# A twelve-sublayer decoder on one core: TensorE's filler products are taken out

## The reference, cut to what matters

```
x = x + sublayer(layernorm(x))
```

## Time and profile before

| what | value |
|---|---|
| median of 3 runs | 4220.63 us (4219.37 to 4225.47) |
| the profiled execution | 4219.39 us, span 4217.6 us |
| PE busy (share of the span) | 3372.7 us (80%), 18289 products |
| DVE, ACT, POOL busy | 2078.1, 1146.6, 401.5 us |
| mean granted TensorE clock | 0.892 |
| filler products (L108) | 1016, 280.9 us busy |
| one batch of the early loop | 727.0 us (777.57 to 1504.55) |
| one batch of the late loop | 249.3 us (3474.11 to 3723.42) |

### The profile page before, as it was taken

How to read it: one execution, slowest core, us unless ns; L and a number is a source line. 1 busy time by engine, 2 the same in 40 slices (tenths; PEclk the granted TensorE clock), 3 DMA queues, 4 the chain that set the end, 5 groups by cost and what they waited for, 6 DMA issues and landing times. The chain is left out here.

```text
span 4217.6 us, 49409 instructions
## 1 busy us (share of the span) xinstructions
PE 3372.7 (80%) x18289; PEld 2170.9 (51%) x18289; DVE 2078.1 (49%) x4553; ACT 1146.6 (27%) x2199; POOL 401.5 (10%) x381
## 2 busy tenths in 40 slices
PE   4778799678869967887986778798595888878888
PEld 3364555436455544655454455544594454554545
DVE  3665446465555556555555655555112535444253
ACT  1413225141222514122341312243131213112121
POOL 0010101010010101001010100101102000010100
PEclk9888899888989978898997889899797898989989
DMA  4000100200010020001001000100683110202011
GB/s 167 13 13 21 64 11 1 87 13 13 21 64 11 8 81 13 13 21 64 11 28 60 13 13 28 57 11 30 248 304 113 52 42 1 85 8 85 8 52 39
DMA packets 53212, 209.29 MB, mean 50 GB/s; under 512 B 4976, under 2 KB 37616, under 8 KB 41328
## 3 DMA queue, kind: packets, MB, share of 16 engines
q1 hardware_dynamic: 48128, 198.85, 12.6%
q0 software_dynamic: 1536, 4.20, 0.3%
q10 hardware_dynamic: 3312, 3.02, 0.2%
HBM read 186.89 MB, written 19.16 MB: 49 GB/s over the span
## 5 line engine op out<-in xcount | busy, mean ns | idle before, releaser
L641 DVE TENSOR_REDUCE nmax<-psum 128x1 f32<-128x512 f32 (+3 forms) x768 | 392.1, 552 | 133.7 <-PE psum L577 91.3
L683 ACT ACTIVATE probs<-psum 128x1024 f32<-128x1024 f32 (+3 forms) x384 | 304.4, 814 | 429.2 <-PE psum L605 290.1
L108 PE MATMUL psum<-select 128*128 128x512 f32 x1016 | 280.9, 431 | 83.0 <-PEq L120 83.0
L572 PE MATMUL psum<-ks,qs 64*128 64x512 f32 (+3 forms) x768 | 212.0, 548 | 139.6 <-DVE nmax L641 123.7
L108 PEld LDWEIGHTS psum<-select 128*128 128x128 f32 x1016 | 206.4, 209 | 157.2 <-issue 113.4
L316 ACT ACTIVATE xc<-psum 128x256 f32<-128x256 f32 x152 | 54.4, 389 | 813.2 <-PE psum L309 813.2
L265 POOL TENSOR_SCALAR rstd<-mean_var 128x4 f32<-128x4 f32 x48 | 11.0, 229 | 2416.8 <-DVE mean_var L290 2416.8
L572 PEld LDWEIGHTS psum<-ks,qs 64*128 64x128 f32 x768 | 89.2, 228 | 288.3 <-DVE nmax L641 267.6
L1488 ACT ACTIVATE exps<-exps,nmax 128x512 f32<-128x512 f32 x256 | 183.4, 717 | 71.4 <-DVE nmax L1434 70.9
L1434 DVE CUSTOM_DVE_ANT_0 exps<-psum,mrows 128x512 f32<-128x512 f32 x256 | 166.1, 689 | 67.8 <-PE psum L1381 64.5
L600 PE MATMUL psum<-qs,ks 64*128 64x512 f32 (+3 forms) x768 | 164.4, 434 | 7.8 <-ACT probs L683 7.8
(11 more groups left out here) (371 smaller groups left out, 6678.9 us busy)
## 6 DMA issues: line engine op xcount, KB each, us to landing
arena<-in_w SPq DMA_DIRECT2D x23, 1028.0 KB, 5.0
arena<-in_w SPq DMA_DIRECT2D x23, 1024.0 KB, 5.2
arena<-in_pack_L_ffn SPq DMA_DIRECT2D x4, 5184.5 KB, 15.2
arena<-in_pack_L_xattn SPq DMA_DIRECT2D x4, 4744.0 KB, 13.9
arena<-in_pack_L_ffn SPq DMA_DIRECT2D x4, 4120.0 KB, 12.9
arena<-in_pack_L_attn SPq DMA_DIRECT2D x5, 2432.0 KB, 9.1
arena<-in_pack_L_attn SPq DMA_DIRECT2D x9, 1280.0 KB, 5.5
arena<-ternary SPq DMA_DIRECT2D x4, 2056.0 KB, 7.8
```

Source lines behind the costliest of these rows:

```text
L108: pe.matmul(self.psum[:, bank, :], self.select[:, 0, :], self.select[:, 0:BANK // P, :], start=True, stop=True)
L572: mm = pe.matmul(net.psum[:, bank_of(s + j), 0:w], qs[half, p, qt * P:(qt + 1) * P], ks[half, p, 0:w], start=True, stop=not causal)
L641: dve.tensor_reduce(nmax[:, p, qt, n % 2:n % 2 + 1], net.psum[:, bank_of(s), 0:w], AX.X, ALU.max, negate=True).then_inc(row_read, 1)
L683: act.activation(probs[:, n % buffers, :, lo:T], net.psum[:, first:first + 2, lo:T], ACT.Exp, scale=scale)\
```

## The change

The counts in line 41 become zero. Nothing else is edited; `keep_warm` is still called, and issues no product.

```diff
-WARM_LAYERNORM, WARM_RECIPROCAL, WARM_ROUTER, WARM_SOFTMAX = 12, 8, 12, 0
+WARM_LAYERNORM, WARM_RECIPROCAL, WARM_ROUTER, WARM_SOFTMAX = 0, 0, 0, 0
```

## The result

The changed kernel takes 4329.66 us (median of 5 runs, 4326.72 to 4331.81), the kernel before 4219.37 us beside it (5 runs, 4218.23 to 4225.47): a ratio of 1.0257, interval 1.0243 to 1.0271, 110 us slower. The forecast was 4309 us with a range of 4262 to 4347. The profiled execution has a span of 4324.9 us, 107.3 us over that of before.

What follows compares the result with a forecast made beforehand. The prediction took TensorE's clock, repeatedly granted only 1.2 GHz, as the limit. Fillers lie in waits that DVE ends; emptied waits make stages start cold at 1.96 us each. Terms sum to 88.5 us, giving 4309 us, range 4262 to 4347.

Steps and rivals of the forecast that it cites:

- L0_ffn's router: 4 groups whose fillers end last: 1.5 us won without them, 7.8 lost as L951 starts cold, 6.3 us in all.
- warm reciprocal waits: Rival: the clock holds through the emptied reciprocal waits, so 31.4 us are not lost; 4278 us, chance 0.13.
- shallow starts: Rival: transposes ahead of a stage bring the clock back, so a start costs 0.7 us; 4252 us, chance 0.07.
- a gain from late fillers: Rival: fillers on the path at batch starts and routers cost 8.7 us, empty waits nothing; 4212 us, chance 0.04.
- Starts all as deep as 0.65: Rival: every cold start is as deep as the two at 0.65, 2.80 us each; 4347 us, chance 0.12.
- Transposes of the layernorms: In six layernorms a batch the last transpose pair comes 0.22 us later, 5.3 us at most; taken as 4.
- Batch starts: L0_attn and L3_attn, 8 groups: transposes start earlier but cold, then the dense stage starts cold; 1.1 and 1.6, 10.8 us.
- L3_ffn: Its layernorm, 6.9 us for a short product run cold, and its router, 9.6 us for cold transposes and dense stage.
- L1_xattn and L3_xattn: Their layernorms, 8 groups: the dense stage behind, warm now, starts cold at 1.96 us each, 15.7 us.
- Already-cold starts: 24 groups whose stage behind starts cold already: 43.2 us now, 47.0 at 1.96 each, so 3.8 us more.
- Reciprocals: 16 groups: the stage behind, at 1.00 now, starts cold at the full price of 1.96 us each, 31.4 us.
- L1801's wait of 3.31 us: Counterexample in the trace before the change: the clock stayed at 1.00 behind this idle TensorE wait.

Runs made afterwards that it cites:

- e1: The kernel before with only the 8 products beside each reciprocal removed (16 groups): 4248.84 us, ratio 1.0063.
- e2: The kernel before with only the 12 products of the layernorms and of L2_attn removed (52 groups): 4274.78 us, ratio 1.0125.
- e6: The kernel after with the 12 products put back in the layernorms of L0_attn and L3_attn alone: 4307.24 us, ratio 1.0208 to the kernel before.
- e10: The kernel before with two VectorE copies, 1.4 us, added ahead of the statistics of L0_attn and L3_attn: 4234.83 us, ratio 1.0030.
- e9: The kernel after with two VectorE copies, 1.4 us, added ahead of the statistics of L0_attn and L3_attn: 4335.60 us, ratio 1.0258 to the kernel before.
- e8: The kernel before with more fillers, also in waits that had none, but none added at the batch change: 4160.49 us, ratio 0.9848.
- e7: The kernel before with half of each filler count (6 in a layernorm, 4 at a reciprocal, 6 in a router): 4307.78 us, ratio 1.0204.

## Why the prediction was right, and which terms were off

The mechanism held. Nearly all the fillers lay inside waits that DVE ends, and taking them out shortened only L0_ffn's router, as forecast. The emptied waits brought 0.5 for the stages behind. DVE's rows kept their lengths, the mean clock fell below 0.88, and the rise went to the length of TensorE's products. Of the rivals, warm reciprocal waits fall by e1 (27 us by the medians); shallow starts (4252) by the newly cold rows at 0.62 to 0.79; a gain from late fillers by the sign. Starts all as deep as 0.65 (4347) lie 17 us above the result, no farther than the forecast below it (21): L951, L1_attn and both stages of L0_attn are at 0.61 to 0.66, the other eight rows at 0.70 to 0.81, so the truth is between the two. The result stands at the upper end of the span that the forecast gave itself (4286 to 4329).

The sum was 19 us too small, by these terms:

- **Transposes of the layernorms, 4 against 14.4.** This is the largest miss, and the table hides it: the forecast's 4.0 stands under "all else", and what the runs show is spread over most rows. The step made only the last pair late, 0.22 us, in six layernorms a batch, 5.3 us at most. L2_ffn's layernorm, second batch, in the kernel before and in the kernel after:

```profile
1476.59 1.41 PE L309 MATMUL psum<-consts,xn 128*128 128x128 f32 x8 [0.62 <-DVE xn L293]
1478.04 0.42 DVE L297 COPY xc<-psum 128x256 f32<-128x256 f32 x1 [0.53 <-PE psum L309]
...
1506.99 1.97 PE L309 MATMUL psum<-consts,xn 128*128 128x128 f32 x8 [4.41 <-DVE xn L293]
1509.00 0.42 DVE L297 COPY xc<-psum 128x256 f32<-128x256 f32 x1 [1.09 <-PE psum L309]
```

VectorE normalises its four tiles in 1.38 us in both. The eight warm transposes keep up with it; the cold ones take 1.97 us and fall behind at every tile, so the copy behind them comes 0.56 us later. Between the tiles and VectorE's next instruction the six named layernorms lost 9.2 us, all twelve 14.4. With the fillers left in the layernorms (e1) it is 0.0, without them (e2) 15.0.

- **Batch starts, 10.8 against 16.0 by the traces and 19.7 by e6.** Two misses partly cancel here: L0_attn cost 14.8 us, forecast 4.4, and L3_attn 1.2, forecast 6.4. For L0_attn the step took half a cold start, "with part of the cold time spent on the transposes". The rows show two losses: L199 needs 10.11 us for 7.11, a loss of 3.0 by itself, and L346 behind it starts deeper than before (0.63 for 0.79). The upper bound of 1.96 was too low, since it held one stage. At L3_attn the first products lost 6.0 us, about as forecast, but 5.9 came back behind them, where L469, cold already, reads 0.79 for 0.65. The Trainium skill, TensorE: Matmul & The Clock Gate, Part 4, PE-mode transpose, says that transposes do not count as activity for the clock. By that rule the term would have been 15.7; that is near 16.0 only as a sum, since it has 7.8 for each of the two starts. The rows do not bear the rule out as it stands: L199 stays cold for long behind its eight transposes, but in the 32 transposes of L1135 the clock rose in the kernel after, too, as in the earlier trace rows. The stretch of L1135 and the 8 us from L469, in the kernel after:

```profile
1236.90:1242.40 5.50, 5.43 (x32) 5.18 (x32) 3.13 (x6) 4.21 (x6) 1.69 (x2) 0.67 0.01 1
...
3580.81:3588.81 8.00, 8.00 (x28) 6.45 (x29) 5.43 (x8) 3.76 (x7) 0.48 (x2) 0.79 0.01 2
```

- **L3_ffn, 16.5 against 23.0.** The product of four instructions costs 3.59 - 1.88 = 1.71 us, as forecast (1.72). Not priced were the eight small products behind it (1.93 us; 1.07 in the kernel before), 0.86 us in each batch. L2028 costs 1.12 - 0.66 = 0.46 us, forecast 0.44. L2043's stage costs 2.4, forecast 1.96. The remaining 1.3 us are the transposes above.
- **L1_xattn and L3_xattn, 15.7 against 18.0.** The starts cost 15.4 us, as priced, and the transposes 2.6. For L1_xattn the reason was incomplete: e10 shows that its 12 products did not secure the clock.
- **Already-cold starts, 3.8 against 7.1.** The transposes make 6.2 of this. What is left, 0.9, is a balance of large moves, with L1_attn at +6.3 and L2_xattn at -3.7 in all. The step priced them by the rows of one batch. e9 moves L1_attn by 4.7 us the other way with a delay of 1.4 us, so these are sizes of the moment.
- **L0_ffn's router, 6.3 against 8.4.** L951 follows VectorE 0.4 to 0.5 us sooner in three batches, 1.3 us won where 1.5 was forecast; its start at 0.66 then costs some 2.4 us, in place of 1.96.
- **Reciprocals, 31.4 against 31.5.** The price of 1.96 us, a mean over nine other stretches, is what a reciprocal start costs (31.5 / 16 = 1.97). That is in part luck: by the forecast's own working the sixteen stages, at 0.62 to 0.80, read 2.19 us, and the runs do not show why 0.2 of it does not reach the path.

Counted as evidence against the mechanism was L1801's wait of 3.31 us. It was no exception to be voted down: the three rows of L346 show that a wait of that size sometimes passes. The prediction called the emptied waits at least as long as the cold ones, but 3.47 us at the reciprocal lies between the 3.31 that passed and the 3.54 that did not. The full price there was a bet; it came in at all sixteen places, in e1 and in the kernel after.

The Trainium skill, TensorE: Matmul & The Clock Gate, Part 1, puts the ramp penalty below 1% of a typical kernel's span. This kernel is not such a one: it pays a ramp behind many waits, the 77 emptied ones make 2.6%, and the kernel before still carried at least 1.5%, which e8 took back.

## What to carry to other kernels

What a filler is worth is read from the work behind its wait, the short transposes as well as the dense stage: the transposes were over half of what the forecast missed. Fill the whole wait: half the products kept a fifth of the gain, and narrow ones none. Ask which instruction ends the block; a filler that ends after it costs the time by which it is late, as at the batch change. Before a few microseconds at one place are credited to an edit, delay the program by about one microsecond and see how far that place moves by itself.

## What the runs showed of the hardware that was not expected

- The same wait of 3.54 us left the products behind it at a mean clock of 0.63, 0.79 and 1.00 in three kernels whose block is the same, and in e9 at different clocks from batch to batch.
- Eight products of 16 columns in a wait left the clock as an empty wait does (L728 3.78 us in both).
- A wait of 2.34 us behind four products of 512 columns left L728 at 2.41 to 3.68 us in the sixteen places of e7; one of 1.43 us behind eight left it at 1.98 in all sixteen of the kernel before.
- A clock that had fallen came back in 32 transposes with nothing else on TensorE, in the kernel after as in the kernel before.
